# A transformer layer with routed experts: the second norm's rows and the second gate's exponential move to ScalarE for seven batches

## What is computed

```
x = x + proj(causal_attention(norm(x)))          16 heads of 8 channels
z = norm(x)                                      the second norm, here called z
logits = z @ Wg                                  8 experts
two largest logits -> softmax over the two -> times alpha[expert]
x = x + sum over the 2 experts of  gate * (gelu(ln_e(z) @ fc1[e] + b1[e]) @ fc2[e] + b2[e])
```

## Time and profile before

| what | us |
|---|---|
| three runs | 544.63, 540.61, 540.32 |
| median | 540.61 |
| span of the profiled execution, first to last instruction | 560.3 |
| attention stage in the profile | 0 to about 368.7 |
| expert stage and the last sums in the profile | from there to the end |

### The profile page before, as it was taken

The page is one execution under the profiler, slowest core; times in us unless marked ns, Lnnn a source line. Parts: engine busy times, 40 slices in busy tenths (PEclk is TensorE's granted clock), DMA queues, the critical chain, the costliest instruction groups (busy, mean ns, idle before and its releaser), DMA issues.

```text
span 560.3 us, 11807 instructions
## 1 busy us (share of the span) xinstructions
PE 473.9 (85%) x3296; PEld 277.1 (49%) x3296; DVE 373.1 (67%) x1316; ACT 322.9 (58%) x661; POOL 366.1 (65%) x712
## 2 busy tenths in 40 slices
PE   3379999999999998998898988786992999999930
PEld 1134443543443453443444443364981888888920
DVE  4588878889889889889889997741543521222226
ACT  2137786776676776676676666752550555565610
POOL 5956676586986986987887876955556444445520
PEclk9589999999999999999999999897996899999985
DMA  2323133134233234234224212276642685666439
GB/s 62 93 57 105 65 93 109 58 105 118 68 101 117 78 87 129 73 91 130 75 66 130 71 40 79 79 236 213 219 159 86 213 264 180 216 194 187 154 129 328
DMA packets 52726, 70.83 MB, mean 126 GB/s; under 512 B 11063, under 2 KB 38430, under 8 KB 52662
## 3 DMA queue, kind: packets, MB, share of 16 engines
q1 hardware_dynamic: 47478, 59.19, 34.7%
q0 software_dynamic: 4320, 8.53, 4.5%
q10 hardware_dynamic: 864, 2.36, 1.2%
HBM read 36.49 MB, written 20.94 MB: 102 GB/s over the span
## 4 chain that ended last, share of the span: by engine, by line
PE 51%; DVE 17%; issue 8%; POOL 6%; SPq 5%; DMA 4%; another core or an unknown queue 4%; ACT 3%; ACTq 0%; DVEq 0%; POOLq 0%
PE acc_bank L748 10%; PE slots L739 10%; PE slots L648 7%; PE acc_bank L680 7%; PE slots L665 5%; SPq L496 4%; DVE masked L940 3%; PE misc L616 3%; POOL z_dram L1235 2%; DVE z L893 2%; DVE row_max L934 2%; POOL probs L1252 2%; DMA y_in<-y_dram 2%; PE slots L644 2%
## 5 line engine op out<-in xcount | busy, mean ns | idle before, releaser
L811 ACT ACTIVATE probs<-slots 128x512 f32<-128x512 f32 (+1 forms) x352 | 185.6, 562 | 86.0 <-PE slots L665 79.2
L940 DVE CUSTOM_DVE_ANT_0 masked<-slots,causal_row 128x512 bf16<-128x512 f32 (+1 forms) x256 | 148.9, 614 | 20.8 <-PE slots L648 20.7
L648 PE MATMUL slots<-stack_k,stack_q 125*128 125x256 bf16 (+3 forms) x512 | 128.5, 307 | 19.4 <-DVE row_max L940 7.5
L1252 POOL TENSOR_SCALAR_AFFINE_SELECT probs<-probs 128x128 f32<-128x128 f32 (+2 forms) x352 | 116.1, 350 | 41.3 <-ACT probs L811 37.4
L665 PE MATMUL slots<-stack_q,stack_k 128*128 128x256 bf16 (+3 forms) x512 | 125.6, 301 | 2.9 <-DVE row_max L934 1.5
L1282 POOL DMA_INDIRECT y_dram<-y,z_in x71 | 69.7, 982 | 73.4 <-DVE y L1126 56.8
L841 ACT ACTIVATE hidden<-slots,w_in 128x256 f32<-128x256 f32 (+1 forms) x156 | 63.1, 455 | 82.6 <-PE acc_bank L748 29.2
L680 PE MATMUL acc_bank<-probs,v 128*32 128x512 f32 (+3 forms) x1024 | 95.6, 447 | 3.4 <-POOL probs L1252 2.7
L648 PEld LDWEIGHTS slots<-stack_k,stack_q 125*128 125x128 bf16 x512 | 48.3, 99 | 95.4 <-DVE row_max L940 49.7
L1235 POOL DMA_INDIRECT z_dram<-z,pos x64 | 63.6, 994 | 32.1 <-DVE pos L1034 17.7
L748 PE MATMUL acc_bank<-hidden,w_in 128*128 128x256 f32 (+1 forms) x312 | 73.0, 376 | 7.8 <-issue 4.0
(11 more groups left out here) (168 smaller groups left out, 523.1 us busy)
## 6 DMA issues: line engine op xcount, KB each, us to landing
w_in<-in_wpack SPq DMA_DIRECT2D x39, 516.0 KB
o_dram<-oT SPq DMA_DIRECT2D x32, 256.0 KB, 2.3
stack_k<-parts SPq DMA_DIRECT2D x95, 64.0 KB
stack_q<-parts SPq DMA_DIRECT2D x93, 64.0 KB
z_in<-z_dram SPq DMA_DIRECT2D x32, 132.0 KB
xt<-in_x SPq DMA_DIRECT2D x8, 256.0 KB, 3.7
onT<-o_dram SPq DMA_DIRECT2D x8, 256.0 KB
o_inv<-inv_dram SPq DMA_DIRECT2D x8, 256.0 KB
```

What stands on the lines that cost most here:

```text
L648: mm = pe.matmul(cols[:, i, :], q[0:K1, hh, blk * P:blk * P + P], k[0:K1, hh, 0:w], start=len(heads) == 1, stop=True, skip_group_check=True)
L811: act.activation(probs_of(n), columns(n, slot), ACT.Exp, scale=SCALE).then_inc(s_exp, 1)
L940: dve.tensor_tensor_reduce(out=masked[:, n % MASKED, 0:w], in0=slots[:, slot, 0:w], in1=causal_row[:, T - w:T], scale=1.0, scalar=NEG, op0 ...
L1252: pool.affine_select(out=diag, in_=diag, compare_op=ALU.is_ge, fill=0.0, base=0, pattern=[[0, len(heads)], [1, P]], channel_multiplier=-1) ...
```

## The change

For batches 0 to 6 the rows of `z` are made by ACT as `rstd * x + (-mean * rstd)`, from a per-token shift that DVE makes in a new stage `r_shift`, one position ahead of `r_z`. The product `ratio` moves from behind the rows into that stage. The exponential of the second gate moves from POOL (as a power of e) to ACT (as Exp). Batch 7 keeps DVE for the rows and POOL for the exponential; it too makes the shift, which nothing reads. In the diff the first two functions are ScalarE's, the next two VectorE's, the last GpSimd's.

```diff
-ROUTE = (("r_stats", 102), ("r_agg", 105), ("r_root", 105), ("r_z", 109), ("zT", 112), ("gate", 114), ("r_top", 118),
+ROUTE = (("r_stats", 102), ("r_agg", 105), ("r_root", 105), ("r_shift", 108), ("r_z", 109), ("zT", 112), ("gate", 114), ("r_top", 118),
          ("r_exp", 119), ("r_copy", 114), ("r_comb", 122), ("rank", 124))
...
-          (6, "r_agg"): 10, (6, "r_root"): 8, (6, "r_z"): 8, (6, "zT"): 3, (6, "gate"): 3,
+          (6, "r_agg"): 10, (6, "r_root"): 8, (6, "r_shift"): 8, (6, "r_z"): 8, (6, "zT"): 3, (6, "gate"): 3,
...
-                "r_z": 13, "zT": 15, "gate": 17, "r_top": 18, "r_exp": 19, "r_copy": 16, "r_comb": 21, "rank": 22,
+                "r_shift": 13, "r_z": 13, "zT": 15, "gate": 17, "r_top": 18, "r_exp": 19, "r_copy": 16, "r_comb": 21, "rank": 22,
...
+            def make_z(b):
+                if b == B - 1:
+                    return
+                wait(act, s_shift, b + 1)
+                wait(act, s_disp[b % 2], 16 * 2 * NT * (b // 2))
+                for n in range(NT):
+                    last = act.activation(z[:, b % 2, 0, n, 0:C], xt[:, NT * b + n, :], ACT.Identity,
+                                          scale=rstd_two[:, 0, n:n + 1], bias=shift[:, n:n + 1])
+                last.then_inc(s_z, 1)
+
+            def second_gate(b):                             # ScalarE
+                if b == B - 1:
+                    return
+                wait(act, s_diff, b + 1)
+                act.activation(second[:, :], diff[:, :], ACT.Exp).then_inc(s_second, 1)
...
+            def find_shift(b):
+                wait(dve, s_rtwo, b + 1)
+                dve.tensor_tensor(ratio[:, :], var_two[:, 0, :], rstd_two[:, 0, :], ALU.mult).then_inc(s_ratio, 1)
+                wait(dve, s_z, b)
+                dve.scalar_tensor_tensor(shift[:, :], mean_var[:, :, 0], -1.0, rstd_two[:, 0, :], ALU.mult, ALU.mult)\
+                   .then_inc(s_shift, 1)
+
             def make_z(b):    
-                wait(dve, s_rtwo, b + 1)
+                if b < B - 1:
+                    return
                 wait(dve, s_disp[b % 2], 16 * 2 * NT * (b // 2))
                 normalise(z[:, b % 2, 0, :, 0:C], xt[:, NT * b:NT * b + NT, :], rstd_two[:, 0, :]).then_inc(s_z, 1)
-                dve.tensor_tensor(ratio[:, :], var_two[:, 0, :], rstd_two[:, 0, :], ALU.mult).then_inc(s_ratio, 1)
...
             def second_gate(b):
-                if b == 0:
-                    pool.wait_ge(s_masks, 1)
+                if b < B - 1:
+                    return
+                pool.wait_ge(s_masks, 1)
                 wait(pool, s_diff, b + 1)
                 pool.tensor_tensor(second[:, :], euler[:, :], diff[:, :], ALU.pow).then_inc(s_second, 1)
```

More of the change, by code:

```diff
@@ L270, in build @@
         ratio = sb("ratio", [P, NT])
+        shift = sb("shift", [P, NT])
         z = sb("z", [P, 2, 2, NT, ROW])
@@ L379, in build @@
         s_ratio = sem("s_ratio")
+        s_shift = sem("s_shift")
         s_diff, s_second, s_comb = sem("s_diff"), sem("s_second"), sem("s_comb")
@@ L852, in _ @@
                   "zT": lambda b: copy_misc(("zT", b), zT[:, :]),
-                  "r_copy": copy_z, "turn_z": turn_z, "fc1": fc1})
+                  "r_z": make_z, "r_exp": second_gate, "r_copy": copy_z, "turn_z": turn_z, "fc1": fc1})
         @block.vector
@@ L1137, in _ @@
                   "pass1": pass1, "maxT": turn_max, "o_invert": invert, "o_scale": scale_o, "proj": project_out,
-                  "r_stats": stats1, "r_agg": aggregate_two, "r_z": make_z, "gate": gate, "r_top": top_two,
+                  "r_stats": stats1, "r_agg": aggregate_two, "r_shift": find_shift, "r_z": make_z, "gate": gate, "r_top": top_two,
                   "r_comb": combine, "rank": put_places, "t_count": count_tiles, "t_span": span_tiles,
```

## The result

The changed kernel takes 550.0 us (median of 5, 549.4 to 553.4), the kernel before 540.6 us on the same chip: a ratio of 1.0167, 95% interval 1.0132 to 1.0203. Forecast were 541.6 us and a range of 537.6 to 546.0. The kernel is slower by 9.4 us, outside the range.

A forecast was written before the change was run, and what follows sets the result against it. PE was taken as the bound, busy for 92% of a middle batch, with DVE close behind. -0.6 us for batches 0 to 5 and +1.6 for batch 6, added to the 540.6 us median, gave 541.6 us; range 537.6 to 546.0.

The forecast's parts named there:

- The step that failed: DVE, batches 0 to 5: ratio 0.35 us and shift 0.2 us, ready before ACT needs it, so no wait.
- the forecast's own sum: Whole kernel: -0.6 us for batches 0 to 5 and +1.6 for batch 6, added to the median: 541.6 us.
- What an instruction costs on ACT: ACT's four row instructions: 0.37 us each in a row, 1.59 us until the last is ready; bounds 0.26 and 0.48.
- The sum of batches 0 to 5: Attention batches: ACT's queue takes nearly all DVE gives back; a gain of 0.10 us a batch, 0.6 for six.
- I count 0: Second gate's Exp on ACT: waits 0.5 us, delays what follows about 0.7, covered by ACT's idle time; cost 0.
- Batch 6: Attention's end: ACT stands still 4.2 us for the shift, PE's gate waits 1.6 us longer, added in full.
- the second rival: Attention's end: ACT's standstill delays the gate 1.6 us, two more half-clock stretches add 3.4 us; 545.0 us, chance 0.15.
- ACT hiding everything: First rival, rows on ACT: 0.26 us an instruction, six batches give 3.2 us, batch 6 costs 1.15; 538.5 us, chance 0.18.
- DVE as the true bound: Third rival, seven batches: DVE's freed time comes back whole, 1.71 us each, 12 us; 528.6 us, chance 0.03.
- The table switch: Fourth rival, batch 6: Exp behind the first Gelu brings two more loads of 1.3 us; 544.2 us, chance 0.04.
- stretches in which all engines stand: Expert stage: stretches without known releaser, longest 11.64 us, taken as much of the profiled span's 19.7 us over the median.

The follow-up runs named there:

- the fastest kernel: The kernel before with DVE's rows two positions later, `zT` and the gate one later, batch 6 as it was: 538.0 us, ratio 0.994.

## Why the prediction was wrong, point by point

**The step that failed.** "`ratio` stays but is made a position sooner (0.35 us), and the shift is new ... which are my bounds; I take 0.2 us." The two together were to take 0.55 us and took 2.1, and ACT, for which "the wait costs nothing here", waited 1.11 us. The prices came from rows that stood at another place. The prediction says of the rows that "one of them stands beside POOL's 1.16 us subtraction"; I read it as the reason why the rows took 2.06 us, and did not ask what else of DVE, moved to a position ahead of the rows, would stand beside the two subtractions. By the timeline of before, the ratio at 198.24 falls right into the first of them:

```profile
198.01 1.15 POOL L1244 TENSOR_TENSOR parts<-qk,parts 128x512 bf16<-128x512 f32 x1
...
199.13 1.16 POOL L1244 TENSOR_TENSOR qk<-qk,parts 128x512 f32<-128x512 f32 x1
```

So the ratio would have ended with the first at 199.16 and the shift with the second at 200.29, and ACT, ready for the rows at 199.12, would have waited 1.2 us; it waited 1.11 in after. The upper bound of 0.35 us was false for that reason, and the trace of before held a better one. Another DVE operation on 128x4, in batch 6, ends with the addition of POOL beside which it starts, at 370.03 and 369.99 (DVE, then POOL):

```profile
368.79 1.24 DVE L1010 TENSOR_SCALAR denom<-second 128x4 f32<-128x4 f32 x1 [0.58 <-POOL second L1191]
```

```profile
368.74 1.25 POOL L1276 TENSOR_TENSOR xt<-xt,bp_s 128x512 f32<-128x512 f32 x1
```

As an estimate, six batches times the 1.2 us that the shift one position ahead gives back put the forecast's own sum at 541.6 + 7.2 = 548.8 us.

The Trainium skill has the rule, on the page "SBUF — State Buffer", section "Who interferes with whom": VectorE in a 2-port mode, or with two SBUF inputs while the GpSimd operation reads SBUF, shares a port pair that is locked, and the second to issue waits for the first to finish. The trace agrees: 0.98 and 1.20 us with ends 0.02 and 0.03 us behind POOL's. I weighed another page of the Trainium skill instead, "ScalarE: Activation LUTs", section "What ACT_TABLE_LOAD costs". Its figures give an estimate of 0.39 us for each of four in a row, and the trace agrees with that too: (1.65 - 0.48) / 3 = 0.39.

**What an instruction costs on ACT.** Called the number on which the forecast rests: 0.48 alone and 1.59 us for four. Measured 0.48 and 1.65 us, the next instruction 1.56 behind the first, not 1.48. Right but for 0.08 us. The 0.06 us for a semaphore stood without a row; in after ACT's rows start 0.02 us behind the shift's end, and the gate 0.05 behind that of `zT`.

**The sum of batches 0 to 5.** -0.6 us forecast. With the shift out of the way (made on POOL) it is under +0.02 in a middle batch and +0.2 from the first to the sixth rank; the mechanism (ACT's queue eats what DVE gives back, the gate hangs on `zT`) is as told. With DVE's wait for POOL it is +6.4 between the same ranks.

**The exponential, "I count 0".** It costs 0.2 us a batch, through a path that I had not seen: ACT later, POOL's cut later, DVE's gate product held behind it. What I had looked for, PE short of a bank, does not occur.

**Batch 6.** This is the second step that failed. ACT's idle time of "4.2 us" was 4.69, and the shift and the ratio took 0.15 us each here, with no wait for POOL. But the forecast let the gate wait for ACT's queue, 1.6 us longer, "added in full". The gate came 2.4 us later, counted from the sixth rank, and PE did not wait for it; the piece is 3.4 us longer, and 2.9 of them are PE's own work at half clock. That is what the second rival named. It added two stretches at half clock for 3.4 us, and there were 6.8 us more at half, worth 2.9. Its 1.6 us for the gate are not there beside them: PE's waits grew by 0.5. So this rival, priced at 545.0 us, had the mechanism of batch 6, but the other two thirds of the loss, in the batches before, are not in it.

**The other rivals.** ACT hiding everything, and DVE as the true bound: no middle batch got shorter. The table switch: the Exp of batch 6 at 377.84 us stands ahead of the one load at 379.93. It did not happen.

**Left open.** What the stretches without a releaser in the expert stage are. They come with one chip's runs (and the profile of before), whatever the kernel. The prediction called them stretches in which all engines stand; that is wrong, for in the 11.64 us of the earlier trace rows POOL is busy for 8.90 and DVE for 5.21. Also open is which wait of PE brings the long stretch at half clock in batch 6, and where the 0.8 us a batch go that the rows on ACT lose without POOL's subtractions, beyond the 0.4 us of the gate's wait. And what is best: later rows on DVE and sooner rows on ACT give 42.6 us a batch each, and no run joins the later rows with other moves.

## What to carry to other kernels

Before an operation is moved or added on DVE, look at what POOL runs at that moment. A 128x4 operation of 0.15 us cost up to 1.2 us there, and when it waits for a result of POOL it can meet whatever POOL does next; make such numbers on POOL behind the result, or put them where POOL does short work.

A row that is slower than its siblings may be a saving by itself. Four instructions that take 1.20 us at one place and 2.06 at another don't ask for another engine, they ask for the better place in the list: two positions later gave 0.6% where the move to ACT lost 1.7%.

Where work runs out, as at the end of the attention, look at PE's busy time and granted clock before counting waits. Here most of what batch 6 lost was the same work of PE at half clock.

## What the runs showed of the hardware that was unexpected

- A DVE operation on 128x4 with two SBUF inputs, 0.15 to 0.16 us alone, lasted until POOL's running instruction ended: 0.98 and 1.20 us beside subtractions, 0.59 beside a 512-wide cut. So did one on 128x4 with a single tensor input, 1.24 us. Row maxima that read PSUM didn't wait: in the fastest kernel one starts at 197.03 and one at 197.64, in the middle of subtractions that run without a gap from 196.22 to 198.50, and they took 0.68 and 0.69 us, as elsewhere.
- On POOL a multiplication of 128x4 takes 0.20 us, the power on 128x8 1.68.
- After a PE wait of 2.45 us, and while it waited 1.66 us again, the granted clock fell to 0.50 and stayed there for 10.2 us, though PE was busy for 9.32 of them. A wait of 2.38 us alone, in the kernel before with later rows, went with 3.4 us at 0.50.
